# Masked scores of the last stage: mask, query scale and row maximum in one VectorE operation per head

## The reference, cut to what matters

```python
def _layer(x, wqkv, qs, ksc, wo, lg, lb, w1, b1, w2, b2):
    h = shift_token(x)
    q, k, v = jnp.split(h @ wqkv, 3, axis=-1)          # 8 heads of 64
    q = l2norm(q) * qs
    k = l2norm(k) * ksc
    q, k = rotary_xpos(q, k)
    o = local_attention(q, k, v)                       # windows of 64 tokens
    x = x + o @ wo
    ...                                                # shift, layer norm, gated feed-forward
# local_attention:
    sim = jnp.einsum('bhwid,bhwjd->bhwij', bq * 8.0, bk)
    mask = (i < j) | (i > j + WINDOW) | (j == -1)
    sim = jnp.where(mask, -jnp.finfo(sim.dtype).max, sim)
    attn = jax.nn.softmax(sim, axis=-1)
    out = jnp.einsum('bhwij,bhwjd->bhwid', attn, bv)
```

## Time and profile before

| what | us |
|---|---|
| median of 3 runs | 2151.02 (2146.39 to 2151.92) |
| the profiled execution | 2162.77 |
| its span in the profile | 2160.8 |
| mean granted clock of TensorE in it | 0.953 of full speed |
| last stage, first product to the end of the span | 1660.8 to 2160.8 |

### The profile page before, as it was taken

One profiled execution on the slowest core, in us unless ns is written; L12 is line 12 of the kernel. 1 busy time (PEld: TensorE's weight loads), 2 busy tenths in 40 slices (PEclk: granted clock), 3 DMA queues, 4 the chain that ended last, 5 costly groups with the idle time before them and its releaser, 6 DMA issues. The chain is left out here.

```text
span 2160.8 us, 40582 instructions
## 1 busy us (share of the span) xinstructions
PE 1943.4 (90%) x9574; PEld 1244.2 (58%) x9574; DVE 1721.3 (80%) x4049; ACT 1633.7 (76%) x5245; POOL 1269.7 (59%) x2141
## 2 busy tenths in 40 slices
PE   4999999999999999999999778669995899999996
PEld 2455555555555555555555546335663677777775
DVE  4799999899979998999999552567886677777774
ACT  3688888888878888888888523279991688888884
POOL 2367677667756766767676633518894545444550
PEclk9799999999989999999999879769997999999999
DMA  1000000000000000000000041112232000000000
GB/s 47 1 1 4 2 20 2 5 9 13 4 2 17 4 4 3 20 2 4 12 9 1 1 141 52 41 32 87 90 106 76 1 1 1 1 1 1 1 1 20
DMA packets 30366, 45.41 MB, mean 21 GB/s; under 512 B 9337, under 2 KB 21889, under 8 KB 29809
## 3 DMA queue, kind: packets, MB, share of 16 engines
q1 hardware_dynamic: 28864, 40.00, 5.9%
q0 software_dynamic: 1248, 2.59, 0.4%
HBM read 38.82 MB, written 5.32 MB: 20 GB/s over the span
## 5 line engine op out<-in xcount | busy, mean ns | idle before, releaser
L405 ACT ACTIVATE a_prob<-a_scores,a_negmax 128x256 f32<-128x256 f32 x1536 | 704.9, 477 | 132.0 <-DVE a_negmax L506 109.6
L506 DVE TENSOR_REDUCE a_negmax<-a_scores 128x2 f32<-128x512 f32 x768 | 521.7, 680 | 77.7 <-PE a_scores L628 62.4
L628 PE MATMUL a_scores<-a_km,a_qT 32*128 32x512 f32 x1536 | 444.2, 657 | 17.5 <-issue 8.9
L639 PE MATMUL a_heads<-a_prob,a_diag 128*128 128x256 f32 x1536 | 404.6, 397 | 43.2 <-DVE a_acc L514 41.3
L639 PEld LDWEIGHTS a_heads<-a_prob,a_diag 128*128 128x128 f32 x1536 | 278.6, 194 | 192.2 <-issue 96.8
L308 POOL TENSOR_TENSOR a_diag<-ident,a_rowinv 128x256 f32<-128x256 f32 x384 | 244.0, 635 | 181.9 <-DVE a_rowinv L547 174.4
L405 ACT ACTIVATION_READ_ACCUMULATOR a_prob<-a_scores,a_negmax 128x1 f32 x1536 | 322.1, 210 | 0.0
L628 PEld LDWEIGHTS a_scores<-a_km,a_qT 32*128 32x128 f32 x1536 | 117.5, 187 | 145.0 <-issue 110.6
L1424 DVE TENSOR_TENSOR_SCAN c_state<-c_decay,c_psD 128x1024 f32<-128x1024 f32 x64 | 146.1, 2286 | 35.6 <-PE c_psD L1541 35.0
L1257 POOL TENSOR_TENSOR c_du<-c_state,c_c_row 128x1024 f32<-128x1024 f32 x64 | 151.2, 2364 | 30.2 <-DVE c_state L1424 20.8
L1882 ACT ACTIVATE d_prob<-d_psS,d_bias,d_inv 128x128 f32<-128x128 f32 (+1 forms) x256 | 122.2, 487 | 27.6 <-DVE d_bias L2016 27.1
(11 more groups left out here) (291 smaller groups left out, 4172.1 us busy)
## 6 DMA issues: line engine op xcount, KB each, us to landing
c_c_row<-c_rows SPq DMA_DIRECT2D x32, 512.0 KB, 3.6
a_w<-in_a_w SPq DMA_DIRECT2D x12, 256.0 KB, 2.6
b_w<-in_b_w SPq DMA_DIRECT2D x1, 2816.0 KB, 14.2
a_rows<-in_a_rows SPq DMA_DIRECT2D x12, 128.0 KB, 2.0
b_w<-in_b_w SPq DMA_DIRECT2D x1, 1536.0 KB, 17.3
d_wqkv<-in_d_wqkv SPq DMA_DIRECT2D x2, 768.0 KB, 5.8
b_rows_in<-in_b_blank SPq DMA_DIRECT2D x1, 1518.0 KB, 8.8
b_packed<-b_rows_in SPq DMA_DIRECT2D x5, 264.0 KB, 4.2
```

Source lines behind the costliest of these rows:

```text
L405: ins = a.activation(prob[part % RING][:, c, :], psS[part % 2][:, c, :], ACT.Exp, bias=negmax[part % 2][:, c:c + 1], accum_out=rowsum[part ...
L506: v.tensor_reduce(negmax[part % 2][:, hs], psS[part % 2][:, hs, :], AX.X, ALU.max, negate=True).then_inc(s["negmax_ready"], 1)
L628: p.matmul(psS[part % 2][:, h * BH:(h + 1) * BH, :], qT[u][rows, t * P:(t + 1) * P], km[u][rows, c:c + BH, :], start=True, stop=True)\
L639: ins = p.matmul(psH[:, t, :], diag[part % RING][:, h, :], prob[part % RING][:, h * BH + 1, :], start=(j == 0 and h == 0), stop=(j == HG - ...
```

## The change

The mask is no longer multiplied in on TensorE. It stays in float32, with the sign turned (0 or +1e25), and the query tables are negated, so that the bank holds minus the scores. For each head VectorE runs one fused operation over the bank: (score + mask) x `inv`, written back to the same place, and at the same time the minimum of the row, begun at 3e38, into `bias`. In the instruction list it appears as an `ISA` row and a second `ISA` row of one column that reads the accumulator out. ScalarE then takes exp(-1.0 x value + `bias`). The semaphore `max_step`, the tile `negmax`, the bfloat16 mask and the two casts are gone. `schedule_d` is the same in both files: no step changes its place.

```diff
-MASKED = -1e25
+MASKED = 1e25
+LARGEST = 3e38
@@ exps, ScalarE
-                                           bias=bias[n % 2][:, j:j + 1], scale=inv[q % 2][t][:, 0, h:h + 1],
+                                           bias=bias[n % 2][:, j:j + 1], scale=-1.0,
@@ start, VectorE
-                chain.link(v.tensor_copy(mask[:], maskf[:]))
-                chain.link(v.tensor_copy(identb[:], ident[:]))
@@ score, VectorE
-                        v.tensor_reduce(negmax[n % 2][:], psS[n % 2][:, :, k0:k1], AX.X, ALU.max, negate=True)\
-                            .then_inc(s["max_step"], 1)
-                        v.wait_ge(s["max_step"], n + 1)
                         v.wait_ge(s["inv_ready"], 2 * q + t + 1)
-                        v.tensor_tensor(bias[n % 2][:], negmax[n % 2][:],
-                                        inv[q % 2][t][:, 0, hh[0]:hh[1] + 1], ALU.mult)\
-                            .then_inc(s["bias_ready"], 1)
+                        for j, h in enumerate(hh):
+                            part = psS[n % 2][:, j, k0:k1]
+                            ins = v.tensor_tensor_reduce(part, part, mask[:, P * t + k0:P * t + k1],
+                                                         inv[q % 2][t][:, 0, h:h + 1], LARGEST, ALU.add, ALU.min,
+                                                         accum_out=bias[n % 2][:, j:j + 1])
+                        ins.then_inc(s["bias_ready"], 1)
@@ score, TensorE
-                        m0 = P * t
-                        p.matmul(out, identb[:], mask[:, m0 + k0:m0 + k1].unsqueeze(1)
-                                 .broadcast_to([P, 2, k1 - k0]), start=True, stop=True)
-                        p.matmul(out, qT[q % 2][:, c, t * P:(t + 1) * P], kT[q % 2][:, c, :, k0:k1], start=False,
-                                 stop=True, skip_group_check=True).then_inc(s["s_full"], 1)
+                        p.matmul(out, qT[q % 2][:, c, t * P:(t + 1) * P], kT[q % 2][:, c, :, k0:k1], start=True,
+                                 stop=True).then_inc(s["s_full"], 1)
@@ layout_d
-    tab = np.stack([QK_SCALE * cos * scale, QK_SCALE * sin * scale, cos / scale, sin / scale])
+    tab = np.stack([-QK_SCALE * cos * scale, -QK_SCALE * sin * scale, cos / scale, sin / scale])
```

More of the change, by code:

```diff
@@ L12 @@
 F32 = mybir.dt.float32
-BF16 = mybir.dt.bfloat16
 U32 = mybir.dt.uint32
@@ L1686, in stage_d @@
         rot = [sb(f"rot{l}", [P, 4, TPS, DHD]) for l in range(DEPTH)]
-        maskf = sb("maskf", [P, L + P])
-        mask = sb("mask", [P, L + P], BF16)
-        identb = sb("identb", [P, P], BF16)
+        mask = sb("mask", [P, L + P])
         down = sb("down", [P, 2, P])
@@ L1700, in stage_d @@
         kT = [sb(f"kT{u}", [P, CD, 2, L]) for u in range(2)]
-        negmax = [sb(f"negmax{u}", [P, 2]) for u in range(2)]
         bias = [sb(f"bias{u}", [P, 2]) for u in range(2)]
@@ L1723, in stage_d @@
                  "o_full", "o_free", "square_ready", "rope_ready", "ss_ready", "inv_ready", "qk_ready", "pool_step",
-                 "max_step", "bias_ready", "rowinv_ready", "hn_ready",
+                 "bias_ready", "rowinv_ready", "hn_ready",
                  "gelu_ready", "mid_ready", "x_ready", "reduce_done")
@@ L1784, in _ @@
             def _(sp):
-                for dst, name in ((tables, "d_tables"), (maskf, "d_mask"), (down, "d_down")):
+                for dst, name in ((tables, "d_tables"), (mask, "d_mask"), (down, "d_down")):
                     sp.dma_start(dst[:], d[name]).then_inc(s["const_in"], 16)
```

## The result

| | before | after | ratio of the runs, 95% interval |
|---|---|---|---|
| first comparison, 4 runs each | 2148.8 | 2131.51 (2128.78 to 2137.44) | 0.9925 [0.9903, 0.9946] |
| repeated, 35 and 12 runs | 2142.14 | 2132.23 (2126.37 to 2142.27) | 0.9955 [0.9938, 0.9971] |
| last stage in the profiles | 515.9 | 504.5, repeated 501.9 | |
| repeat of a unit in them | 28.91 | 28.16, repeated 28.16 | |

Times are us. The change makes the kernel faster, by 17.3 us in the first comparison and by 9.9 in the larger one. The last stage is taken from its first memset (1644.9 us before, 1630.7 after) to the end of the span.

What follows compares the result with a forecast made beforehand. Bound: a last-stage chain through TensorE, then ScalarE and VectorE, not TensorE alone. Steady units -6.1, first units -0.4, start -0.8, last unit -0.9 sum to -8.2 us, from 2151.02 to 2142.8; range 2137 to 2158.

Steps and rivals of the forecast that it cites:

- D: VectorE in the last stage: increase per score step from fused operations and accumulator reads, taken as 0.14 us.
- rival 1: VectorE: the fused operation is cheap, D = 0, giving 2137.4 us; chance 0.12.
- (a): Shift of L2060's start per unit (one sequence of one layer): ScalarE alone after two score steps, -0.92 + 2D.
- (b): Shift of L2060's start per unit: VectorE waits for ScalarE's square, then a third score step; -0.93 + 3D, deciding at -0.51 us.
- Four leave the chain, 0.49: TensorE: four of a unit's eight mask products lie in the chain's first half, so removing them saves 0.49 us.
- the 0.36 of the sum: ScalarE, second half of a unit: two exponential pairs, each 0.18 us shorter without the scale column.
- The casts: Start of the last stage: two casts of mask and identity, ahead of all TensorE work there, go away: -0.8 us.
- L1985's wait for the square: Sign on VectorE: its wait for ScalarE's square after the first exponential pair gets shorter than 0.52 us.
- rival 3: VectorE: fused operation takes two cycles a column, D = 0.41 and 0.54, giving 2159.7 us; chance 0.21 together with no overlap.
- route (c): Shift of L2060's start per unit: VectorE never waits, four score steps; -1.27 + 4D, deciding from D = 0.31.
- larger fixed price: VectorE: fused operation costs 0.08 us more per head, D about 0.3, no change at 2149.6 us; chance 0.22.
- drain rule: VectorE: next operation starts only once the pipe is empty, no overlap, D = 0.46, 2157.2 us; chance 0.21 shared with rival 3.

Runs made afterwards that it cites:

- e6: Changed kernel with one more VectorE addition of 128 x 70 numbers ahead of each score step: repeat 29.15 us against 28.16.
- e3: Changed kernel with mask products back on TensorE and scale back as a column, so only VectorE's part differs from before: repeat 28.96 us, ratio 1.0001.
- e2: Kernel before with a constant exponential scale in place of the column of inverse norms: repeat 28.56 us, ratio 0.9970.
- e4: Changed kernel with the mask products back on TensorE, nothing else: repeat 28.60 us, ratio 0.9965 to the kernel before.
- e1: Kernel before with the mask products on TensorE left out, scores unmasked: repeat 28.61 us, ratio 0.9987.
- e5: Changed kernel with the exponential's scale read from a column of minus ones again: repeat 28.66 us, ratio 0.9994 to the kernel before.

## Why the prediction was wrong, step by step
**The direction and the chain held.** The gain came from where it was looked for. The profile of the changed kernel follows its chain back only as far as 2068.4 us, so it does not show the steady units; that three score steps stand on the chain is shown by e6, and that it still closes through L2055 by the wait at 1846.99. The forecast of -8.2 us stands against -11.4 and -14.0 in the last stage and -9.9 in the larger comparison; against the -17.3 of the first it is too small by half, and 2131.51 lies below the low end of 2137.

**The level was the first failure.** I added my shift to a median of three runs, 2151.02, and gave the range no room for the scatter between executions. The profiled execution, 11.75 above that median, was a sign of it. Larger sets of the kernel before have medians of 2146.99 (31 runs) and 2142.14 (35 runs), from 2137 to 2160. In the larger comparison the changed kernel's 2132.23 lies 10.6 below the 2142.8 forecast: 8.9 of that is the level and 1.7 the change.

**The size of D was the second, and the first in the mechanism.** The step that failed is "neighbours without a wait overlap: ... 0.08 of it is hidden", applied to the read of the accumulator. The read is hidden whole: the next operation starts with it. The price of the fused operation was right (347 taken, 355 measured; 414 and 422) and that of the read nearly (160 and 141), but in the queue a step became 0.03 shorter for 128 keys and 0.01 longer for 192, and D is 0.0, not 0.14. e3 confirms it with +0.05 a unit, all in the second part, where ScalarE waits out the last read. This was the state that rival 1 described, with its chance of 0.12, for another reason: it had the fused operation cheap. The steady units gave 12 x 0.75 = 9.0, not 6.1.

**With D = 0 the formulas (a) and (b) give -0.92 and -0.93, measured -0.75.** Two terms of them were too large. The first part gave 0.47 (16.72 to 16.25) for a forecast of 0.56: that is the weight load that the mask had covered, 0.08. The second part gave 0.28 (11.50 to 11.22) for 0.36. The first pair of exponentials starts 0.03 later, since ScalarE has to wait out the last read, and the second pair's gain partly goes to a new wait. ScalarE in that stretch:
```profile
1841.46 0.42 ACT L1879 ACTIVATE d_prob<-d_psS,d_bias 128x192 f32<-128x192 f32 x1 [0.94 <-DVE d_bias L2010]
...
1843.88 0.60 ACT L1910 ACTIVATE d_probT<-d_psT 128x512 f32<-128x512 f32 x1
1844.49 1.28 ACT L1927 ACT_TABLE_LOAD   x1
```
Its copy of 1843.88 waits for the transposes that TensorE starts at 1843.24, behind the score product which itself waited 0.46 for a bank. The order of the starts says so, and the other kernels bear it out: the copy stands 0.64 behind those transposes in the three kernels with the constant scale (e2, e4, after) and 0.75 in e1 and e5, where ScalarE is the later one. From the freed bank's first product to the transposes TensorE takes 0.80 with a mask (e4) and 0.72 without: this is the 0.08 that the masks are worth in the second part, a term that I had put at nothing.

**Masks.** "Four leave the chain, 0.49" was wrong for the masks alone (e1: 0.30) and about right with the shorter exponentials beside them (e4 to after: 0.44), though 0.08 of that is a mask of the second part. I had written the wait at the third product down as a help worth 0.07, while without the ScalarE part it costs 0.19.

**Exponentials.** 0.09 each was right. The two pairs of the second part did not give the 0.36 of the sum but 0.23 (e2) to 0.32 (e5 to after); that e2 as a whole gave 0.35 is luck, as said there. That the pair ahead of the third product counts as well stood in my sum in the 0.07 only; it is worth 0.12 with the masks and 0.18 without them.

**The rest.** The casts: the gap from the layer norm's last row to the first memset fell from 1.04 to 0.39 us, 0.65 of the 0.8. The stage up to the first steady unit gave 1.8 and 2.3, forecast 1.2; the last unit 0.5 and 2.6, forecast 0.9, with the granted clock of that stretch inside it. Of the signs, L1985's wait for the square did get shorter (0.33 at 1843.23 for 0.52). TensorE's busy time in the stage fell by 13.9 us (462.05 to 448.18), not 17, and nearly all of it came off the stage's length: only 2.5 us turned into waits, where I had expected most of it to. A slip in rival 3: by the formulas route (c) passes (b) at D = 0.34, not 0.31.

**Rivals.** 2 and 3 are out: no larger fixed price, and 422 - 355 = 67 ns for 64 columns is 1.05 ns a column, that of the maximum in the earlier trace rows and not twice as much. The drain rule of the Trainium skill ("VectorE: DVE Perf Modes", "The DRAIN you can't avoid"), taken without the exception that its section itself points to, would have made the fused step alone cost 3 x 0.46 - 0.19 = 1.19 a unit; e3 measured 0.05. The section "Two Vector instructions with no wait between them" of the same page of the Trainium skill agrees with the starts at 1827.26 and 1840.95.

## What to carry to other kernels
When the repeat of the chain runs through three engines, an engine's saving is worth what it takes out of that loop, and two savings can be worth more together than apart (0.30 and 0.36 here, 0.80 together): look at who waits next for whom at the place where the first one ends. A total that agrees does not show the mechanism (e2 had the right 0.35 from the wrong places): split the repeat at a fixed instruction and compare the parts. For an edit in one stage, compare that stage's length and its repeat in the profiles; a median of three whole executions lay 8.9 us off that of 35 here, more than the 8.2 forecast for the edit, and a range must hold it. Counting operations misleads on VectorE where they follow without a wait: four took the time of two.

## What was not expected of the hardware
- A read of VectorE's accumulator (141 ns) starts together with the next operation and takes no time of the queue (1827.26, 1840.95), while whoever needs its result waits for its end, 0.14 us after the last one started.
- A VectorE addition of 128 x 70 numbers with both inputs in SBUF takes 0.57 us when it starts inside a GpSimd operation of 128 x 512 and 0.23 otherwise (e6). It ends 0.08 to 0.09 after the GpSimd operation, whether that one takes 1.27 us (L1830) or 1.04 (L1839), which looks like waiting for its end; nearly all of them had 0.48 to 0.49 left of it at their start, and the one with 0.13 left (1815.06) took 0.23, so no run separates waiting from being slowed. The fused operation, with one input in PSUM, is not affected: beside such operations it takes 0.35 to 0.36 (128 keys) and 0.42 to 0.43 (192) in the changed kernel.
- Without a product in front that waits in its place, a score product after a wait shows its weight load: 0.51 us for 0.43 (128 keys), with the load at 1803.78 and the product at 1803.81 in e1.
